# GpSimd masks the first group's exponentials of each half in the last many-head stage of a two-layer decoder

## The reference, cut to what matters

```python
mask = (i >= j) & (j != -1)
mask = mask & (req == rek)
bq = _rotary(bq)
bk = _rotary(bk)
p = jnp.einsum('bhnqd,bhnkd->bhnqk', bq, bk) / jnp.sqrt(jnp.asarray(hd, bq.dtype))
p = jnp.where(mask, p, jnp.finfo(p.dtype).min)
a = jax.nn.softmax(p, axis=-1)
o = jnp.einsum('bhnqk,bhnkd->bhnqd', a, bv)
```

## Time and profile before

| what | value |
|---|---|
| median of three runs | 776.32 us (772.29 to 776.37) |
| the profiled execution, its own time | 779.23 us |
| its span, first to last instruction | 777.4 us |
| mean granted TensorE clock | 0.987 |
| busy: TensorE, its weight loads | 742.5 us (96%), 608.0 us (78%) |
| busy: VectorE, ScalarE, GpSimd | 481.2 us (62%), 389.0 us (50%), 297.3 us (38%) |
| stage 4 in the span | 474 to about 645 us |

### The profile page before, as it was taken

The page is one execution under the profiler, slowest core; times in us unless marked ns, Lnnn a source line. Parts: engine busy times, 40 slices in busy tenths (PEclk is TensorE's granted clock), DMA queues, the critical chain, the costliest instruction groups (busy, mean ns, idle before and its releaser), DMA issues.

```text
span 777.4 us, 19012 instructions
## 1 busy us (share of the span) xinstructions
PE 742.5 (96%) x7189; PEld 608.0 (78%) x7189; DVE 481.2 (62%) x1388; ACT 389.0 (50%) x951; POOL 297.3 (38%) x397
## 2 busy tenths in 40 slices
PE   8999999999999999999999999999999899899996
PEld 7887777776788888888888887777867667688885
DVE  4686787887654445356555566787856458554435
ACT  3445677777533233436666544444534266266630
POOL 2323333434224213211212255565656435545540
PEclk9999999999999999999999999999989899999999
DMA  8997244300256642101000021000000101245428
GB/s 310 402 220 145 76 109 117 78 15 2 62 139 165 166 128 70 56 2 30 4 3 3 4 90 51 16 16 16 16 30 16 36 31 41 90 138 155 145 87 320
DMA packets 67962, 69.92 MB, mean 90 GB/s; under 512 B 22721, under 2 KB 58561, under 8 KB 66849
## 3 DMA queue, kind: packets, MB, share of 16 engines
q1 hardware_dynamic: 64464, 59.37, 26.5%
q0 software_dynamic: 3408, 9.34, 3.5%
HBM read 39.03 MB, written 29.40 MB: 88 GB/s over the span
## 4 chain that ended last, share of the span: by engine, by line
PE 77%; DVE 10%; ACT 4%; issue 3%; POOL 2%; DMA 2%; SPq 1%; another core or an unknown queue 1%; DVEq 0%; POOLq 0%
PE pj L403 12%; PE pj L396 8%; PE sc L609 7%; PE ov L622 7%; PE ov L558 6%; PE sc L485 4%; PE sc L514 4%; PE pj L390 4%; PE ov L812 4%; PE sc L462 4%; PE sc L804 3%; DVE mx L1103 3%; PE pj L546 2%; PE sc L535 2%; PE pj L567 2%
## 5 line engine op out<-in xcount | busy, mean ns | idle before, releaser
L1642 ACT ACTIVATE pr<-sc 128x512 f32<-128x512 f32 x128 | 66.1, 606 | 72.9 <-PE sc L514 65.6
L1125 DVE TENSOR_REDUCE mx<-sc 128x4 f32<-128x512 f32 x120 | 74.5, 683 | 23.7 <-PE sc L485 21.5
L1651 ACT ACTIVATE pr<-sc,mx 128x128 f32<-128x128 f32 x256 | 72.9, 379 | 31.4 <-DVE mx L1103 30.3
L1883 POOL TENSOR_SCALAR ve<-mv 128x2 f32<-128x2 f32 x40 | 13.3, 333 | 180.6 <-DVE mv L1038 180.2
L609 PE MATMUL sc<-xnT,W 128*128 128x256 f32 x256 | 61.0, 382 | 0.8 <-DVE mx L1125 0.8
L1700 ACT ACTIVATE hT<-sc,vecs 128x256 f32<-128x256 f32 x64 | 30.1, 475 | 62.6 <-PE sc L609 62.6
L622 PE MATMUL ov<-W,hT 128*128 128x256 f32 x256 | 60.1, 379 | 0.0
L1627 ACT ACTIVATE oT<-ov 128x512 f32<-128x512 f32 x48 | 28.9, 602 | 53.9 <-PE ov L558 48.4
L622 PEld LDWEIGHTS ov<-W,hT 128*128 128x128 f32 x256 | 48.5, 190 | 6.7
L1961 POOL DMA_INDIRECT routed_y<-pr,mask x39 | 37.3, 955 | 41.5 <-DVE mask L1379 34.9
L609 PEld LDWEIGHTS sc<-xnT,W 128*128 128x128 f32 x256 | 47.3, 190 | 7.0 <-DVE mx L1125 1.0
(11 more groups left out here) (259 smaller groups left out, 1794.5 us busy)
## 6 DMA issues: line engine op xcount, KB each, us to landing
sorted_x<-more_xT SPq DMA_DIRECT2D x15, 1152.0 KB, 7.9
kM<-sorted_x SPq DMA_DIRECT2D x39, 129.0 KB
cT<-in_ctxT SPq DMA_DIRECT2D x16, 256.0 KB, 3.6
pr<-kept_at SPq DMA_DIRECT2D x32, 128.0 KB, 3.2
W<-in_w SPq DMA_DIRECT2D x2, 1024.0 KB, 13.5
cT<-in_ctx SPq DMA_DIRECT2D x8, 256.0 KB, 3.8
oT<-kept_at SPq DMA_DIRECT2D x16, 128.0 KB, 3.2
hd<-kept_at SPq DMA_DIRECT2D x16, 128.0 KB, 3.3
```

Source lines behind the costliest of these rows:

```text
L1125: last = v.tensor_reduce(dst, bank[b][:, :].rearrange("p (c i s) -> p c i s", c=C, i=2), AX.X, ALU.max, negate=True)
L1642: a(pr[n % 4][:], four(b), ACT.Exp).then_inc(drained[b], 1)
L1651: last = a(pr[n % 4][:, i, :], bank[b][:, i * S:(i + 1) * S], ACT.Exp, bias=mxg[n % 4][:, i:i + 1])
```

## The change

In stage 4 the first group of each half (n % 4 == 0) gets no mask in its scores. Instead:

- ScalarE's `masked_last` replaces the four `exps`: it copies the first bank as max(-s, 0) into `pr[0]` (so that an unmasked score above zero can't overflow), takes the second group's exponential, then exp(-`pr[0]`) in place, and then the third and fourth groups.
- GpSimd's `shut_out` multiplies `pr[0]` by a table of zeros and ones (`mb0`), one product of 128x512 per half, placed in its list behind `rotate` in both sides.
- VectorE writes that table once, at the end of unit 25, as `mbT1 >= 0`, over the whole of `mb0`.
- TensorE leaves out the preload of that group, and `probs_times_values` takes the groups in the order 1, 2, 3, 0, waiting for GpSimd's semaphore `shut` before group 0.

Two semaphores (`s_eased`, `shut`) are new, two unused ones go.

```diff
@@ by_key (TensorE)
-                    added = masks is not None and n not in DVE_MASKED[masking(U)]
+                    added = masks is not None and n % 4 and n not in DVE_MASKED[masking(U)]
@@ probs_times_values (TensorE)
-                for g in range(4):
-                    pe.wait_ge(*emptied(name, U, 4 * j + g))
+                for g in (1, 2, 3, 0) if U // PAIRS == 4 else range(4):
+                    if U // PAIRS == 4 and g == 0:
+                        pe.wait_ge(shut, 2 * (U - 4 * PAIRS) + j + 1)
+                    else:
+                        pe.wait_ge(*emptied(name, U, 4 * j + g))
@@ alone1 (VectorE)
+                if U == 3 * PAIRS + 1:
+                    v.tensor_scalar(mb0[:], mbT1[:], 0.0, None, ALU.is_ge).then_inc(s_mb, 1)
@@ ScalarE
+            def masked_last(U, j):
+
+                b, k = spot["s", U, 4 * j]
+                act.wait_ge(filled[b], k)
+                a(pr[0][:], four(b), ACT.Relu, scale=-1.0).then_inc(drained[b], 1)
+                exps(U, 4 * j + 1)
+                act.wait_ge(drained[b], k)
+                a(pr[0][:], pr[0][:], ACT.Exp, scale=-1.0).then_inc(s_eased, 1)
+                exps(U, 4 * j + 2)
+                exps(U, 4 * j + 3)
...
-                if shifted(U):
+                if f == 4:
+                    masked_last(U, j)
+                elif shifted(U):
                     for n in range(4 * j, 4 * j + 4):
                         exps(U, n)
@@ GpSimd
+            def shut_out(U, j):
+
+                pool.wait_ge(s_mb, 6)
+                pool.wait_ge(s_eased, 2 * (U - 4 * PAIRS) + j + 1)
+                g.tensor_tensor(pr[0][:], pr[0][:], over(mb0[:, 2 * (U % PAIRS) + j, :], 4), ALU.mult).then_inc(shut, 1)
...
                 if stage(U + 2) == 4:
                     rotate(U + 2, 1)
+                if stage(U) == 4:
+                    shut_out(U, 0)
                 if late(U, 34) is not None:
                     p = late(U, 34)
                     inverse(mv5[p % 2], ve5, rstd5[p % 2], mv5_done, ve5_done, rstd5_done, p)
...
                 if stage(U + 2) == 4:
                     rotate(U + 2, 0)
+                if stage(U) == 4:
+                    shut_out(U, 1)
                 if late(U, 36) is not None:
                     count(late(U, 36))
                     scatter(late(U, 36))
```

More of the change, by code:

```diff
@@ L256, in program @@
         mx_done, ri_done, kM_done, masked_done, s_causT = sems("mx_done ri_done kM_done masked_done s_causT")
+        s_eased, shut = sems("s_eased shut")
         s_shift = sems("s_shift0 s_shift1")
@@ L266, in program @@
             "top5_done tops5_done kept5_done picked_done counted_done")
-        spots_done, first_done, one_done, slot_done = sems("spots_done first_done one_done slot_done")
+        first_done, one_done, slot_done = sems("first_done one_done slot_done")
         den_done, dene_done, deni_done, share_done, comb_done = sems(
             "den_done dene_done deni_done share_done comb_done")
-        cnt_done, step_done, many_done, upto_done, reach_done, behind_done, who_done, base_done, row_done, tab_done = sems(
-            "cnt_done step_done many_done upto_done reach_done behind_done who_done base_done row_done tab_done")
+        step_done, many_done, upto_done, reach_done, behind_done, who_done, base_done, row_done, tab_done = sems(
+            "step_done many_done upto_done reach_done behind_done who_done base_done row_done tab_done")
         s_counts, s_wgu, s_blank, s_init, ids_done, sgt_done, diag_done = sems("s_counts s_wgu s_blank s_init ids_done sgt_done diag_done")
```

## The result

| | before | after |
|---|---|---|
| median of 20 runs each, us | 771.93 (767.37 to 776.81) | 777.60 (774.13 to 779.69) |
| ratio after to before, 95% interval | | 1.0064 (1.0044 to 1.0084) |
| profiled execution, us (span) | 779.23 (777.4) | 778.06 (776.2) |

The change costs 0.64%, that is +4.9 us on 771.9 (the two medians lie 5.7 apart). The forecast was +3.0 us, 779.3 us on the three runs known then, and the time came out at 777.6, inside the range. The likeliest class of the forecast had been a change within 0.5% (0.50), the next one slower by more than that (0.37); it is this second one that the ratio falls in, with the lower end of its interval at 0.44%. The two profiled executions must not be subtracted: that of the kernel before stood 7 us over its own median.

What follows compares the result with a forecast made beforehand. TensorE was taken as the bound, VectorE and GpSimd close behind. Terms -3.5 + 2.1 + 0.6 + 2.0 + 0.4 + 0.7 = +2.3, with unit 39 and late VectorE +3.0 us; on 776.3, 779.3 us, range 772.8 to 784.0.

Steps and rivals of the forecast that it cites:

- Preloads, -3.5 us: One preload matmul fewer in each of the stage's sixteen halves, 0.22 us each: -3.5 us if TensorE alone bounds them.
- ScalarE, +2.1: One more activation per half, not covered in side 1 of units 32 and 38 and both sides of 39: +2.1 us.
- GpSimd's product: One 128x512 product per half, taken as 1.24 us; TensorE waits for it in side 1 of unit 32: +0.6 us.
- Maxima, root and void savings: From unit 34 the product delays the norm's root, then VectorE's maxima and by_key: +2.0 us; two savings void: +0.4 us.
- void in (35,1): Side 1 of unit 35: VectorE is 0.1 us from being the bound, so the preload's 0.22 us saving is void.
- VectorE late: VectorE, already running later, starts side 1 of unit 35 0.3 us late.
- Scatters at the end, +0.7: Side 1 of unit 39: count and four scatters stand behind the product, so GpSimd reaches the last root 0.7 us late.
- rival (c): Scatters of units 38 and 39 move behind the exponentials and can hold the last norm: +1 to +4 us net; chance 0.22.
- Rival (a): GpSimd is done before anyone asks and the savings stay: -3.5 to -3.9 us, 772.4 to 773.3 us; chance 0.17.
- Rival (b): Side 1 of unit 35: the product holds VectorE by their shared port, at most 1.24 us: 780.5 us; chance 0.13.

Runs made afterwards that it cites:

- the control: The kernel before run once more, unedited, against the kernel before: ratio 1.0008, 774.30 us.
- control pair: The kernel before and the changed kernel, each run once more unedited: ratios to before 1.0008 (774.30 us) and 1.0057 (778.17 us).
- the last run: Kernel before plus one wait: in units 36 and 37 GpSimd's scatters wait for the second half's probabilities-times-values product; ratio 0.9921, 766.94 us.
- control of after: The changed kernel run once more, unedited, against the kernel before: ratio 1.0057, 778.17 us.

## Why the prediction was right, and where it was not

**Preloads, -3.5 us.** 36 are left, and each is worth 0.21 us while TensorE is the bound (0.22 forecast). As a sum over sixteen it failed: measured alone 0.0% and 0.2%, so 0 to some 2 us. From (36,1) on the scatters' gaps and the clock behind them move the halves by far more than a preload does.

**ScalarE, +2.1.** (32,1) came as forecast: alone it costs 0.50 us up to (36,1). The term left out the table load of 1.28 us in (39,1), of which 0.6 us shows at the end of the trace and 1.2 us, not resolved, between the medians.

**GpSimd's product.** 1.16 us in place of 1.24. TensorE's wait for it in (32,1) is 0.32 us in place of 0.6.

**Maxima, root and void savings.** For (32,0) to (36,1) the sum holds -2.0 (nine preloads) + 0.49 + 0.6 + 2.0 + 0.2 (void in (35,1)) + 0.3 (VectorE late) = +1.6 us; the profiles show +1.17. Counted from the scores of (32,0), the scores of (33,0) start 0.60 us later than in the first profile of before, those of (34,0) 0.17 (two and more preloads saved since), (34,1) 1.14, (35,0) 0.92, (35,1) 1.25, (36,0) 1.03 and (36,1) 1.17. The large steps up are behind (32,1), behind (34,0) and behind (35,0), the places named. Half by half the sum is within 0.1 us of the profiles (+0.97 us behind (34,0) where it has 1.1 less a preload of 0.22) but for one: from (35,1) to (36,0) it has a void saving and a late VectorE, and the distance fell from 11.48 to 11.26 us, the whole saving of a preload. That is the 0.4 to 0.5 us by which the sum is too high here.

**Scatters at the end, +0.7, and rival (c).** The last root comes with no idle time before it, as forecast, and the time to the end is 138.3 us against 137.0 in the control. But the main price of the late scatters was not there: it lies in PV (38,1), 4.6 to 5.5 us. This is the step that failed: the sum took the stretch from (36,1) on as if the place of the scatters cost TensorE nothing. Rival (c) had the cause, the windows of the scatters, and a net price of +1 to +4 on the sum, but the wrong victim: it looked at late signals to ScalarE and at the last norm, and did not look at TensorE's own instructions. It also had the late windows of units 38 and 39 and missed those of 36 and 37, where the delay helps. The control pair shows both signs, and the last run shows that the helpful one can be had alone.

So it is partly luck that the measured +4.9 us lies near +3.0. In the control pair the late scatters give back 4.7 and 4.3 us behind (36,1) and (37,1) and cost 5.5 behind (38,1), and the halves (37,0), (38,0) and (39,0) are longer by 1.3, 1.2 and 1.1 us. The sum had none of these but 0.2 us in (38,1), and together they come to nothing. The time itself, 779.3 us, came nearer to 777.6 than that because the starting point was 4.4 us too high (776.3 from three runs, 771.9 from twenty) and the increment 2 us too low. Rival (a) is out: VectorE waits for the root in (34,0), (35,0) and (36,0), as named, and by 0.61 us in (37,0) as well, where the prediction had it late enough. Rival (b) is not seen in (35,1), where it was named. VectorE is held beside the product in (37,0) and (38,1), but what that costs was not measured; in (37,0) VectorE comes to wait for the root behind it all the same. And the held VectorE takes back what the root's earlier place gives.

**What stays open.** Why TensorE's issue stalls while the scatters run, no view here shows; GpSimd's work on them and their own transfers (DMA share 0.40 from 620 to 622 us) come together in every run. The Trainium skill, "Runtime: NRT & Kernel Launch", on instruction fetch, says that each engine streams its instructions by a DMA queue of its own, and that this is mostly hidden; that the scatters disturb it would fit, and nothing here tests it. The profile counts packets of the instruction queues: two fall between 573 and 576 us in the control of before and two between 618 and 621 in the control of after, both among the gaps, but two fall between 573 and 574 in the last kernel as well, where there is no gap. Also open is how much of the gaps the kernel before pays in its median: all three profiled executions with its plain schedule took 774.8 to 779.2 us, above their medians, and on the first chip it stood at 767.2, where the changed kernel was not timed. What the change costs on a chip on which the kernel before has no spells is thus not known. The 6 us of the last kernel are shown on one chip. A changed kernel with the scatters of units 38 and 39 first and the table load early was not run.

## What to carry to other kernels

Before a change that lengthens an engine's queue is summed up, list what moves with that queue: here the four scatters behind the new product were worth more than any duration in the sum. When short instructions of one engine show gaps whose releaser is "issue", look at what GpSimd issues beside them, try one wait that moves it over long instructions, and time it. Do not judge such a kernel by one profile of each side; compare distances inside the stage, which repeat to 0.03 us where no scatter runs, and time the rest.

## What the runs showed of the hardware

- Under four scatters (about 5 us of GpSimd) 32 short matmuls took 5.2 us in place of 1.08, from the seventeenth on in bursts of one to four with gaps of 0.3 to 1.0 us; they followed 32 others under the first scatter. Eight matmuls of 256 columns had no gap under scatters, and neither had 32 short ones under the last scatter, behind longer ones.
- Under the scatters of (39,1), in the kernel with late scatters and nothing else, ScalarE started the copy of PV's result 3.0 us behind PV's end (644.36, releaser "remote").
- Behind TensorE being idle for half of 4 us its granted clock stood at 0.50 for about 7 us, a loss of 3.4 us; other spells cost 1.7. In the kernel with late scatters and nothing else, no fall followed the gaps of (38,1). In the last kernel, without those gaps, no spell stands between 570 and 660 us.
- A VectorE copy of 128x2 that starts 0.08 us behind a GpSimd product of 1.17 us lasts 1.12 us in place of 0.18.
- A Relu between a silu and an exponential needs no table of its own, and so lets the exponential's load of 1.28 us slide behind the data it waited for.
